# A selective-scan kernel: VectorE multiplies two neighbouring states with C in one operation instead of two

## What is computed

```
dA = exp(A[channel, n] * dt[channel, t])            # 16 states
dBu = dt * B[n, t] * hs
h[n] = dA * h_before[n] + dBu                       # a scan over time, for each state
y = sum over n of h[n] * C[n, t]                    # then + hs*D, * silu(gate), times Wout
```

## Time and profile before

| | before |
|---|---|
| median of 3 runs | 1075.25 us (1075.24 to 1075.85) |
| the profiled execution | 1076.49 us, of which the span of the core is 1074.7 us |
| VectorE busy | 1016.8 us, 95% |
| GpSimd busy | 891.5 us, 83% |
| ScalarE busy | 828.2 us, 77% |
| TensorE busy | 914.1 us, 85% |
| mean granted TensorE clock | 0.957 |

### The profile page before, as it was taken

The page is one execution under the profiler, slowest core; times in us unless marked ns, Lnnn a source line. Parts: engine busy times, 40 slices in busy tenths (PEclk is TensorE's granted clock), DMA queues, the critical chain, the costliest instruction groups (busy, mean ns, idle before and its releaser), DMA issues.

```text
span 1074.7 us, 14666 instructions
## 1 busy us (share of the span) xinstructions
PE 914.1 (85%) x4328; PEld 562.3 (52%) x4328; DVE 1016.8 (95%) x1214; ACT 828.2 (77%) x1154; POOL 891.5 (83%) x496
## 2 busy tenths in 40 slices
PE   3988888867877997898879979987998799879998
PEld 2756565534444564554445545555555455445554
DVE  7979898699999999999999999999999999999996
ACT  2777877678888865798887658988866689888662
POOL 4444445699999899989998999899989989998993
PEclk9999999979889999899999988999899899999999
DMA  7687768993111218532212183421212922212101
GB/s 282 192 261 245 272 225 316 363 365 133 54 60 40 88 41 274 185 122 74 80 39 88 40 302 140 137 79 59 75 54 70 341 97 101 79 59 79 40 0 40
DMA packets 53157, 150.24 MB, mean 140 GB/s; under 512 B 5728, under 2 KB 14048, under 8 KB 50016
## 3 DMA queue, kind: packets, MB, share of 16 engines
q1 hardware_dynamic: 53088, 149.41, 40.1%
HBM read 111.37 MB, written 38.01 MB: 139 GB/s over the span
## 4 chain that ended last, share of the span: by engine, by line
DVE 42%; issue 28%; PE 13%; ACT 10%; POOL 5%; DVEq 1%; DMA 1%; POOLq 0%; SPq 0%
DVE da L1100 18%; DVE prod L1075 11%; DVE hp L1100 8%; ACT da L994 3%; POOL dt_du L371 3%; PE mm L1135 2%; PE yT L1226 2%; DVE y L1083 2%; ACT L983 2%; ACT L982 2%; POOL hs_lo L366 2%; DVE gate_bf L1113 1%; PE proj L599 1%; PE proj L600 1%; PE proj L601 1%
## 5 line engine op out<-in xcount | busy, mean ns | idle before, releaser
L994 ACT ACTIVATE da<-unit,neg_a 128x512 f32<-128x512 f32 x512 | 338.6, 684 | 157.1 <-DVE prod L1075 154.0
L833 POOL TENSOR_TENSOR dbu<-unit,b_head 128x1024 f32<-128x1024 f32 x192 | 449.4, 2365 | 0.0
L1100 DVE TENSOR_TENSOR_SCAN da<-da,dbu 128x512 f32<-128x512 f32 x352 | 416.7, 1213 | 1.2
L1226 PE MATMUL yT<-ident,prod 128*128 128x128 f32 x1408 | 227.3, 290 | 94.7 <-DVE prod L1075 94.0
L1226 PEld LDWEIGHTS yT<-ident,prod 128*128 128x128 f32 x1408 | 167.8, 147 | 229.4 <-DVE prod L1075 189.9
L1063 POOL TENSOR_TENSOR hp<-hp,c_head 128x512 f32<-128x512 f32 x128 | 163.3, 1276 | 50.7 <-DVE gate_bf L1116 46.2
L1100 DVE TENSOR_TENSOR_SCAN hp<-da,dbu 128x512 f32<-128x512 f32 x160 | 192.6, 1204 | 3.3 <-ACT da L994 3.3
L1075 DVE TENSOR_TENSOR prod<-da,c_head 128x512 f32<-128x512 f32 x256 | 170.2, 665 | 0.0
L1175 PE MATMUL mm<-xn_b,w_sb 128*128 128x512 fp8e4 x512 | 141.9, 409 | 16.5 <-ACT acc L1014 12.9
L833 POOL TENSOR_TENSOR dbu<-unit,b_all 128x1024 f32<-128x1024 f32 x64 | 151.3, 2364 | 0.0
L1187 PE MATMUL mm<-xnT_b,wgate 128*128 128x512 f32 x256 | 128.7, 600 | 0.0
(11 more groups left out here) (118 smaller groups left out, 1285.5 us busy)
## 6 DMA issues: line engine op xcount, KB each, us to landing
unit<-unit_d SPq DMA_DIRECT2D x32, 768.0 KB, 4.4
unit_d<-dt_du SPq DMA_DIRECT2D x32, 512.0 KB, 2.7
wf<-in_wffn SPq DMA_DIRECT2D x12, 1024.0 KB, 6.5
c_head<-bc_d SPq DMA_DIRECT2D x24, 512.0 KB, 4.1
b_head<-bc_d SPq DMA_DIRECT2D x18, 512.0 KB, 4.8
unit_d<-hs SPq DMA_DIRECT2D x32, 256.0 KB, 6.7
w_sb<-w_d SPq DMA_DIRECT2D x64, 128.0 KB, 4.0
wgate<-in_win_gate SPq DMA_DIRECT2D x32, 256.0 KB, 2.8
```

The costliest lines, as they stand in the source:

```text
L833: return nc.gpsimd.tensor_tensor(dbu[:, n % DBUS:n % DBUS + NS, :], twice, b_all[n // NS], ALU.mult)
L994: nc.scalar.activation(da[n % SLOTS][:, :], unit[:, k % 2, 0, :], ACT.Exp, scale=neg_a[:, k, n:n + 1]).then_inc(da_ready, 1)
L1100: nc.vector.tensor_tensor_scan(state, da[n % SLOTS][:, :], dbu[:, n % DBUS, :], 0.0, ALU.mult, ALU.add).then_inc(scanned, 1)
L1226: ins = nc.tensor.matmul(yT[k % 2][:, t * P:(t + 1) * P], product[:, t * P:(t + 1) * P], ident[:, :], start=False, stop=last, is_transpose ...
```

## The change

Two own states that are neighbours, lie in neighbouring PSUM banks and get neighbouring places of the ring `prod` are multiplied in one operation of 128x1024 elements. `TWO` lists the first states of these pairs: (2, 5, 10, 13) in the units k = 0, 1 and 6; (5, 10, 13) in k = 2; (2, 5, 13) in k = 3; (2, 10, 13) in k = 4; (2, 5, 10) in k = 5 and 7: 27 pairs in a batch, 108 in the run. The pair (n, n+1) is written behind scan n+2. The four dA banks become one PSUM tensor, and C of the last four states one SBUF tensor, so that two tiles can be one operand.

```
+TWO = [[n for n in (2, 5, 10, 13)[:4 if k < KU - 1 else 3] if n in OWN[k] and n + 1 in OWN[k] and PROD.slot(k, n) + 1 == PROD.slot(k, n + 1)] for k in range(KU)]
...
-        c_all += [sb(f"c_all{g}", [P, NS, L])[:, :, :] for g in range(G_AHEAD, G)]
+        c_tail = sb("c_tail", [P, (G - G_AHEAD) * NS, L])
+        c_all += [c_tail[:, g * NS:(g + 1) * NS, :] for g in range(G - G_AHEAD)]
...
-        da = [ps(f"da{i}", [P, L]) for i in range(SLOTS)]
+        da_banks = ps("da", [P, SLOTS, L])
+        da = [da_banks[:, i, :] for i in range(SLOTS)]
...
+            def two_times_c(b, k, n):
+
+                slot = PROD.slot(k, n)
+                dve.wait_ge(scanned, (b * KU + k) * N + n + 2)
+                dve.wait_ge(prod_used, PROD.slot_left(b, k, n + 1))
+                if k == 0:
+                    for g in sorted({n // NS, (n + 1) // NS}):
+                        dve.wait_ge(c_loaded[g], b * 16 + 16)
+                of = c_head[:, n:n + 2, :] if n + 1 < G_AHEAD * NS else c_tail[:, n - G_AHEAD * NS:n + 2 - G_AHEAD * NS, :]
+                nc.vector.tensor_tensor(prod[:, slot:slot + 2, :], da_banks[:, n % SLOTS:n % SLOTS + 2, :], of, ALU.mult).then_inc(prod_ready, 2)
...
-                    if n > 0 and n - 1 in OWN[k]:
+                    if n - 2 in TWO[k]:
+                        two_times_c(b, k, n - 2)
+                    elif n > 0 and n - 1 in OWN[k] and n - 1 not in TWO[k]:
                         times_c(b, k, n - 1)
```

More of the change, by code:

```diff
@@ L993, in body @@
                         act.wait_ge(*state_left((u - 1) // KU, before, n - SLOTS + N))
-                    nc.scalar.activation(da[n % SLOTS][:, :], unit[:, k % 2, 0, :], ACT.Exp,
+                    nc.scalar.activation(da[n % SLOTS], unit[:, k % 2, 0, :], ACT.Exp,
                                          scale=neg_a[:, k, n:n + 1]).then_inc(da_ready, 1)
@@ L1074, in times_c @@
                     dve.wait_ge(c_loaded[n // NS], b * 16 + 16)
-                nc.vector.tensor_tensor(prod[:, slot, :], da[n % SLOTS][:, :], c_all[n // NS][:, n % NS, :], ALU.mult).then_inc(prod_ready, 1)
+                nc.vector.tensor_tensor(prod[:, slot, :], da[n % SLOTS], c_all[n // NS][:, n % NS, :], ALU.mult).then_inc(prod_ready, 1)
+            def two_times_c(b, k, n):
[7 more added lines that the diff above has]
+                nc.vector.tensor_tensor(prod[:, slot:slot + 2, :], da_banks[:, n % SLOTS:n % SLOTS + 2, :], of, ALU.mult).then_inc(prod_ready, 2)
             def gated(u, k):
@@ L1095, in body @@
                     dve.wait_ge(dbu_ready, u * N + n + 1)
-                    state = da[n % SLOTS][:, :]
+                    state = da[n % SLOTS]
                     if n in POOLED[k]:
@@ L1099, in body @@
                         state = hp[:, HP.slot(k, n), :]
-                    nc.vector.tensor_tensor_scan(state, da[n % SLOTS][:, :], dbu[:, n % DBUS, :], 0.0,
+                    nc.vector.tensor_tensor_scan(state, da[n % SLOTS], dbu[:, n % DBUS, :], 0.0,
                                                  ALU.mult, ALU.add).then_inc(scanned, 1)
-                    if n > 0 and n - 1 in OWN[k]:
+                    if n - 2 in TWO[k]:
+                        two_times_c(b, k, n - 2)
+                    elif n > 0 and n - 1 in OWN[k] and n - 1 not in TWO[k]:
                         times_c(b, k, n - 1)
```

## The result

| | before | after |
|---|---|---|
| median | 1075.85 us (5 runs, 1075.24 to 1078.3) | 1094.07 us (5 runs, 1092.84 to 1094.85) |
| ratio | | 1.0166, 95% interval 1.0155 to 1.0178 |
| span of the profiled execution | 1074.7 us | 1091.1 us |
| mean granted TensorE clock | 0.957 | 0.955 |

A forecast was written before the change was run, and what follows sets the result against it. VectorE sets the pace, but ScalarE has no slack at each gelu. Median 1075.25 + 17.0 for the late gelu chain - 3.3 saved by pairs = 1088.95, 1089 us; own range 1084.4 to 1092.3, 1084 to 1095 for 8 times in 10.

The forecast's parts named there:

- The reading of the bound: VectorE, 95% busy, sets the pace, but at each gelu ScalarE has no slack: the chains arrive within 0.06 us.
- The slip: At a gelu behind pair (10, 11), exp 15 and scan 1 come 1.06 us late: 16 turns, +17.0 us.
- The waits: VectorE's scan of state 1 waits for ScalarE's dA 20 times, some 21 us in all against 3.3.
- The saving of a pair: On VectorE, one product of 1024 columns costs 1.12 us instead of 1.18 for two, saving 0.055.
- Where savings are lost: Pairs in stretches set by ScalarE, at gelu or `SWITCH`, save nothing; 60 pairs count in the run, -3.3 us.
- What costs nothing: Other exps, TensorE, GpSimd and SyncE's loads were taken to have cover or slack for the later products, adding nothing.
- the feed-forward cover: In units k = 1 to 5, feed-forward operations keep VectorE 1.58 us, giving ScalarE slack before scan 6.
- Rival 3: TensorE, fed two products at once, runs late and delays ScalarE's chain: 9 us, 1098; chance 0.09.

The follow-up runs named there:

- Experiments 1: The changed kernel without the pair (10, 11) in units k = 0, 1, 2 and 4, 92 of 108 pairs kept: 1076.84 us, ratio 0.9999.
- experiment 2: The kernel before with only the pair (10, 11) in units k = 0, 1, 2 and 4, 16 pairs: 1095.84 us, ratio 1.0176.
- 5: The kernel before with only the pair (10, 11) in k = 5, 6 and 7, 12 pairs, no gelu behind: 1077.75 us, ratio 1.001.
- 7/8: The kernel before and the changed kernel, each with a plain copy for the gelu and no table loads around it: 1072.21 us and 1076.43 us.
- experiment 6: The changed kernel, all pairs, with ScalarE's feed-forward copies of k = 0 to 3 one exp earlier: 1098.34 us, ratio 1.0214.
- covered2: The kernel before with 40 pairs: (5, 6) in k = 0 to 3 and 6, (2, 3) in k = 1, 3, 4, 5, (13, 14) in k = 6: 1074.36 us.
- experiment 8: The changed kernel, all pairs, with a plain copy for the gelu and no table loads around it: 1076.43 us, ratio 0.9995.

## Why the prediction held, and which steps were off

**The reading of the bound** held. VectorE is 95% busy and hardly waits, yet at the gelu the chain of ScalarE ends within 0.06 us of it. Experiments 1, 2, 5 and 7/8 show this from four sides: without the 16 pairs all but 1.7 us of the loss is gone, with them alone it is all there, a pair (10, 11) with no gelu behind has no wait, and 2.57 us of slack takes the waits at scan 1 away.

**The slip**, forecast at 1.06 in 16 turns, measured 1.00 to 1.03. What stands in line, exp 14 and its copy, was 1.10. The copy's part of it is shown alone in experiment 6: 0.48.

**The waits** were to be 20, 21 us in all; they are 16, 20.2 us. At the four turns from 3 to 4 ScalarE and VectorE stay within 0.1 us of each other and no wait shows.

**The saving of a pair**, the term that I took at 0.055, is 0.07: the two-bank product costs 1.11 to 1.12 from start to start where two took 1.18. What I took for fixed, 0.59 less 0.533, rested on the columns of another product; the merged products show it directly. The figure of 75 ns that the Trainium skill gives (page "Vector Engine (DVE) Microarchitecture Reference", section 5.2) was the nearer one; covered2 measures 2.63 / 40 = 0.066 a pair.

**Where savings are lost**: as forecast, a pair inside a stretch that ScalarE sets saves nothing. Scan 6 behind `SWITCH` waits up to 0.3 in 11 units of the changed kernel.

**What failed is two sentences of the part "What costs nothing"**. The first: "at the tightest turn it ends at 593.73 and `y_t` starts at 595.13, 1.4 us of slack". I took the tightest deadline of TensorE for `y_t`, and the pair (10, 11) for what makes it late. The deadline that is missed is the next one, the transposes before the gate product of k=6, and what makes TensorE late is (5, 6) of k=5, 1.66 us, because it has hardly a gap from there on. And the end of the kernel stood nowhere in my sum: behind its last product VectorE has only the gate product left and waits 5.47 for TensorE where it waited 4.07, and the end comes 1.33 us later. What makes `y` late at k=7 of two batches (0.25) no run isolates.

The second: "At a turn from k=0 to 1 it was late already, but exp 6 has the feed-forward cover there". The cover isn't enough: experiment 8 shows scan 6 waiting 1.19 there in three batches. In the changed kernel the gelu's wait hides all but 0.14 of it, which is luck and not the forecast.

Rival 3 named TensorE's lateness; its size was 4.8 us and not 9, and most of it reached VectorE at the gate product and not through ScalarE's chain.

**The sum with measured terms**: 16 turns x 1.03 = 16.5; 60 pairs x 0.07 = -4.2; TensorE: at k=6 the step is 0.35 above -0.14 in three batches and 1.21 in the last, at k=7 0.35 above -0.21 in two, at k=1 0.14 too much in three, at the end 1.4: 4.8. Together 17.1, as in stage B. This is an account of the steps, from which its terms are taken, and no second test. By the medians it is 18.2, with an interval of 16.7 to 19.1. The forecast came 3.4 us short of stage B: TensorE's 4.8 was put at nothing, and the slip (0.5 too much) and the saving (0.9 too little) made up for 1.4 of it.

## What to carry to other kernels

Merging two operations of the busiest engine into one saves its fixed cost, here 0.07 us, but it holds the first result back until the second is done, here 1.7 us. Before doing it, ask at each place who takes the first result, what stands in that engine's queue between it and the next thing that the busy engine waits for, and how much slack that chain has; a busy engine with no visible waits may have none. Merge only where those chains have slack (40 of the 108 places are shown to have it here), and look at the end of the program apart, where no busy engine covers anything.

## What I had not expected of the hardware

- VectorE's product over two neighbouring PSUM banks costs nothing extra: 1195 to 1204 ns for 128x1024, against means of 664 to 670 for 128x512, and 1.11 to 1.12 us from start to start.
- TensorE's granted clock fell to half for some 3 us behind a wait of 2.12 us at the same turn of two batches of experiment 2 (two pairs of matmuls took 1.60 and 1.91 instead of 1.02), and a step that is 1.10 without it became 2.79. The wait alone doesn't decide it: behind two other waits of 2.12 in the same profile the granted clock was 1.00. So what a later input of TensorE costs can differ by 1.7 us between batches of one run.
- Stage A of the same code ended anywhere from 218.8 to 223.7 us, while units of stage B that an edit doesn't touch repeat to 0.01 us. Differences of 2 us in the whole time could be read only in stage B alone.
